# Low-pass block, 16 images: x read a second time in 32-token blocks, its transposes on VectorE, and the next image's first pairs between the H filter chunks

## The reference

```python
xs = jnp.einsum('bhwc,dc->bhwd', x, W1) + b1      # 768 -> 192 channels
xs = jax.nn.gelu(xs, approximate=False)
xs = fft_low(xs)          # |inverse FFT of (FFT * centred low-pass mask)| over H and W
xs = jnp.einsum('bhwd,cd->bhwc', xs, W2) + b2     # 192 -> 768 channels
return x + xs
```

## Time and profile before

| | us |
|---|---|
| median of the runs shown | 2677.9 |
| the runs | 2672.61, 2677.9, 6215.89 |
| profiled execution, from first to last instruction | 2680.7 |
| PE busy in it | 2549.4 (95%) |
| VectorE busy | 1833.9 (68%) |
| ScalarE busy | 1350.4 (50%) |
| GpSimd busy | 397.9 (15%) |
| DMA queue, share of 16 engines' span | 59.8% |

### The profile page before, as it was taken

How to read it: one execution, slowest core, us unless ns; L and a number is a source line. 1 busy time by engine, 2 the same in 40 slices (tenths; PEclk the granted TensorE clock), 3 DMA queues, 4 the chain that set the end, 5 groups by cost and what they waited for, 6 DMA issues and landing times.

```text
span 2680.7 us, 53277 instructions
## 1 busy us (share of the span) xinstructions
PE 2549.4 (95%) x16864; PEld 2485.4 (93%) x16864; DVE 1833.9 (68%) x3980; ACT 1350.4 (50%) x3077; POOL 397.9 (15%) x500
## 2 busy tenths in 40 slices
PE   8899898998999989899998999989999899998999
PEld 7799898998989989899898999989999899998999
DVE  6487575775758757587675766757667576675767
ACT  5355454554545545455454545545455454554544
POOL 1102021020211202112020120201202012020120
PEclk9899999999999999999999999999999999999999
DMA  6474664746647466474665846558455584555845
GB/s 207 106 252 138 201 242 114 264 129 200 240 114 261 131 198 242 114 273 129 204 230 129 282 116 215 208 135 298 103 211 202 140 300 99 207 204 145 299 102 221
DMA packets 342566, 509.48 MB, mean 190 GB/s; under 512 B 78418, under 2 KB 210770, under 8 KB 342228
## 3 DMA queue, kind: packets, MB, share of 16 engines
q1 hardware_dynamic: 342228, 505.31, 59.8%
HBM read 253.60 MB, written 251.66 MB: 188 GB/s over the span
## 4 chain that ended last, share of the span: by engine, by line
PE 83%; DMA 6%; SPq 4%; issue 3%; DVE 2%; ACT 2%; DVEq 0%; ACTq 0%
PE ps L400 22%; PE ps L385 12%; PE ps L401 10%; PE ps L472 6%; PE ps L462 6%; PE ps L463 5%; PE ps L469 5%; PE ps L466 5%; DMA xt_hi<-filtered_rows 4%; PE ps L437 3%; SPq L317 2%; PE ps L411 2%; PE ps L445 2%; DMA filtered_rows<-filt 2%; PE ps L413 2%
## 5 line engine op out<-in xcount | busy, mean ns | idle before, releaser
L400 PE MATMUL ps<-w1s,xt_hi 128*128 128x384 f32 x3072 | 980.2, 374 | 0.0
L521 ACT ACTIVATE xt_hi<-ps 128x512 fp32r<-128x512 f32 x768 | 457.7, 598 | 697.8 <-PE ps L385 674.5
L401 PE MATMUL ps<-w1s,xt_lo 128*128 128x192 f32 x3072 | 772.3, 251 | 0.0
L640 DVE TENSOR_TENSOR xt_lo<-ps,xt_hi 128x512 fp32r<-128x512 f32 x768 | 529.8, 691 | 282.4 <-ACT xt_hi L521 279.6
L702 DVE TENSOR_TENSOR xs<-ps,xs 128x384 f32<-128x384 f32 x1024 | 564.5, 556 | 210.9 <-PE ps L472 159.8
L401 PEld LDWEIGHTS ps<-w1s,xt_lo 128*128 128x128 f32 x3072 | 588.0, 191 | 0.0
L400 PEld LDWEIGHTS ps<-w1s,xt_hi 128*128 128x128 f32 x3072 | 578.8, 188 | 0.0
L472 PE MATMUL ps<-w2b_hi,ob 128*128 128x384 f32 x1024 | 357.0, 349 | 42.7 <-DVE ob L693 42.7
L763 POOL TENSOR_TENSOR diff<-hid 128x192 f32<-128x192 f32 x240 | 232.2, 967 | 1016.8 <-ACT hid L529 1016.8
L462 PE MATMUL ps<-w2a_hi,oa_hi 128*128 128x384 f32 x1024 | 361.3, 353 | 20.8 <-DVE xs L702 19.7
L385 PE MATMUL ps<-ident,xs 128*128 128x128 f32 x2304 | 344.1, 273 | 11.2 <-DMA xs<-x_dram 10.6
(11 more groups left out here) (62 smaller groups left out, 3051.3 us busy)
## 6 DMA issues: line engine op xcount, KB each, us to landing
out_dram<-xs SPq DMA_DIRECT2D x127, 1536.0 KB, 9.3
xs<-x_dram SPq DMA_DIRECT2D x80, 1536.0 KB, 7.2
filtered_rows<-filt SPq DMA_DIRECT2D x256, 192.0 KB, 2.0
x_tail<-x_dram SPq DMA_DIRECT2D x32, 1536.0 KB, 8.5
xs<-x_dram SPq DMA_DIRECT2D x32, 768.0 KB, 6.3
xt_hi<-filtered_rows SPq DMA_DIRECT2D x64, 256.0 KB, 5.1
cols_b<-filtered_rows SPq DMA_DIRECT2D x128, 128.0 KB, 5.4
xt_lo<-filtered_rows SPq DMA_DIRECT2D x64, 256.0 KB, 6.4
```

The costliest lines, as they stand in the source:

```text
L400: nc.tensor.matmul(ps_h[t % 2][:, 0:2 * D], hi, w1s[:, k, :], start=k == 0, stop=False)
L401: ins = nc.tensor.matmul(ps_h[t % 2][:, D:2 * D], lo, w1s[:, k, 0:D], start=False, stop=k == KC - 1)
L521: nc.scalar.activation(xt_hi[:, n % XT_SLOTS, :], ps_xt[n % 2][:], ACT.Copy).then_inc(s_xhi, 1)
L640: nc.vector.tensor_tensor(xt_lo[:, n % XT_SLOTS, :], ps_xt[n % 2][:], xt_hi[:, n % XT_SLOTS, :].bitcast(F32), ALU.subtract).then_inc(s_xlo, 1)
```

## The change

x is read twice. The first reading (`load_xq`) goes into `xq`: for each pair of tiles four DMAs, each into 32 partitions. Partition 32j+t holds token t of each of the pair's eight blocks of 32 tokens, with the 192 channels of quarter j, so pieces of 768 bytes. One VectorE transpose of 128 x 768 per tile then turns every 32 x 32 block and leaves channels on the partitions in `xt`; PE no longer transposes, the identity matrix is gone, and W1 is laid out in the matching order. ACT rounds `xt` into `xt_hi` and DVE subtracts, both from SBUF, a whole tile of 768 elements at a time. The second reading (`load_xr`) brings the same tokens, pair by pair, in an eight-slot ring `xr` in which they are added and stored; the copies of the tail tiles are gone.

`hid_sum` and `hid_pre` work on a pair, `add_half` becomes `add_tile`. `hid_lo` and the low part of the first 128 channels of y (`split_a_lo_pair`) move from VectorE to GpSimd; all twelve stores of y are ScalarE's. The scratch rows get one tensor per image, so that rows of the next image can be written while columns of this one are read. The order becomes: for r in 0 to 15, stage A of pair r+3 of image i with stage C of pair r of image i-1; then the four H chunks of image i, with stage A of pairs 0, 1 and 2 of image i+1 behind the first three of them.

The diff, cut to its core:

```diff
-BLOCKS = 4
-UNITS = TILES * KC // BLOCKS
...
+B = 32
+QUADS = P // B
+CQ = C // QUADS
+
+LEAD = 3
+XQ = 4
+XT = 4
+XR = 8
+X_AHEAD = 5
...
+    x_q = x.rearrange("b h w c -> b (h w) c").rearrange("b (m g t) c -> b m t g c", g=2 * QUADS, t=B)
...
-    rows = nc.dram_tensor("filtered_rows", (H, W, D), F32, kind="Internal").ap()
+    rows = nc.dram_tensor("filtered_rows", (IMAGES, H, W, D), F32, kind="Internal").ap()
...
+            def load_xq(i, p):
+                if p >= XQ or later(i):
+                    sp.wait_ge(s_t, TILES * i + 2 * (p - XQ) + 2)
+                for j in range(QUADS):
+                    sp.dma_start(xq[j * B:(j + 1) * B, p % XQ, :, :].rearrange("p t (g c) -> p (t g) c", c=CQ),
+                                 x_q[i, p, :, :, j * CQ:(j + 1) * CQ]).then_inc(s_xq[p % XQ], 16)
+
+            def load_xr(i, p):
+                if p >= XR or later(i):
+                    sp.wait_ge(s_out[p % XR], 16 * (2 * i + p // XR))
...
+                sp.dma_start(xr[:, p % XR, :, :], x_i[:, 2 * p:2 * p + 2, :]).then_inc(s_xr[p % XR], 16)
...
@@ SyncE @@
+            def turn(i, a, c, n):
+                for r in range(PAIRS):
+                    q = r + LEAD
+                    if a and q < PAIRS:
+                        feed(i, q, n)
+                    if c and 3 <= r < 3 + PAIRS - XR:
+                        load_xr(i - 1, r + X_AHEAD)
+                    if c and r >= 1:
+                        store(i - 1, r - 1)
+                    if a and r >= PAIRS - X_AHEAD:
+                        load_xr(i, r - (PAIRS - X_AHEAD))
+                    if a and q < PAIRS:
+                        write_rows(i, q - 1)
+                    if a and q == PAIRS:
+                        write_rows(i, PAIRS - 1)
+                        read_cols(i)
...
+            def mm1_tile(i, t):
...
+                pe.wait_ge(s_xlo, TILES * i + t + 1)
+                if t % 2 == 0 and (t > 0 or later(i)):
+                    pe.wait_ge(s_pre, PAIRS * i + t // 2)
...
+            def mm1_pair(i, q):
+                for t in range(2):
+                    mm1_tile(i, 2 * q + t)
+                if q >= 1:
+                    filter_w_pair(i, q - 1)
+
@@ TensorE @@
+            def turn(i, a, c, n):
+                for r in range(PAIRS):
+                    q = r + LEAD
+                    if a and q < PAIRS:
+                        mm1_pair(i, q)
+                    if c:
+                        out_tile(i - 1, 2 * r)
+                    if a and q == PAIRS:
+                        filter_w_pair(i, PAIRS - 1)
+                    if c:
+                        out_tile(i - 1, 2 * r + 1)
+                    if a and r == PAIRS - 2:
+                        corner_sums(i)
+                for k in range(CHUNKS):
+                    if a:
+                        for v in range(YBANKS):
+                            filter_h_item(i, k, v)
+                    if n and k < LEAD:
+                        mm1_pair(i + 1, k)
...
+            def transpose_tile(i, t):
+                q = t // 2
+                if t % 2 == 0:
+                    dve.wait_ge(s_xq[q % XQ], 16 * QUADS * (PAIRS // XQ * i + q // XQ + 1))
+                nc.vector.transpose(xt[:, t % XT, :], xq[:, q % XQ, t % 2, :]).then_inc(s_t, 1)
+
+            def xt_lo_tile(i, t):
+                dve.wait_ge(s_xhi, TILES * i + t + 1)
+                nc.vector.tensor_tensor(xt_lo[:, t % XT, :, :].rearrange("p c (g t) -> p c g t", t=B),
+                                        xt[:, t % XT, :].rearrange("p (g c t) -> p c g t", c=KC, t=B),
+                                        xt_hi[:, t % XT, :, :].bitcast(F32).rearrange("p c (g t) -> p c g t", t=B),
+                                        ALU.subtract).then_inc(s_xlo, 1)
...
@@ VectorE @@
+            def turn(i, a, c, n):
...
+                    if c and r > 0:
+                        add_tile(i - 1, 2 * r - 1)
...
+                    if mid:
+                        feed_lo(i, q, n, 0)
+                        feed_transpose(i, q, n, 0)
+                    if c and r + 1 < PAIRS:
+                        split_b_lo_pair(i - 1, r + 1)
+                    if mid:
+                        hid_pair(i, q)
+                        feed_lo(i, q, n, 1)
+                    if c:
+                        add_tile(i - 1, 2 * r)
+                    if mid:
+                        feed_transpose(i, q, n, 1)
...
@@ GpSimd @@
+            def turn(i, a, c, n):
+                if c:
+                    split_a_lo_pair(i - 1, 0)
+                for r in range(PAIRS):
+                    if c and r + 1 < PAIRS:
+                        split_a_lo_pair(i - 1, r + 1)
+                    if a and r + LEAD < PAIRS:
+                        hidden(i, r + LEAD)
```

More of the change, by code:

```diff
@@ L196, in later, with wrap @@
             return not isinstance(i, int) or i > 0
[L198 to L227, removed]
+        def wrap(i, q, n):
+            if q < PAIRS:
+                return i, q
+            return (i + 1, q - PAIRS) if n else None
         def y_slot(c, v):
@@ new lines, in _, with feed @@
+            const(w1f, w1t.rearrange("p (k d) -> p k d", d=D), s_w1)
+            load_xq(0, 0)
+            for t in range(2):
+                const(b1_rows[:, t, :], b1.partition_broadcast(P), s_b1_rows)
+            load_xq(0, 1)
+            load_constants()
+            for p in range(2, XQ):
+                load_xq(0, p)
+            for q in range(LEAD):
+                load_xq(0, q + X_AHEAD - 1)
+                if q >= 1:
+                    write_rows(0, q - 1)
+            def feed(i, q, n):
+                ahead = wrap(i, q + X_AHEAD - 1, n)
+                if ahead is not None:
+                    load_xq(*ahead)
@@ new lines, in feed @@
+            def feed(i, q, n, k):
+                ahead = wrap(i, q + 1, n)
+                if ahead is not None:
+                    xt_hi_tile(ahead[0], 2 * ahead[1] + k)
+            for t in range(2):
+                xt_hi_tile(0, t)
+            for q in range(LEAD):
+                for k in range(2):
+                    feed(0, q, True, k)
+                if q >= 1:
+                    stage_filtered(0, q - 1)
+                gelu_pair(0, q)
+            set_up_at = {0: set_up_w2a_hi, 1: set_up_w2b_hi, 2: set_up_corner}
@@ L587, in turn @@
                 if a:
[L588 to L590 removed]
                     split_hi_pair(i, 0)
[L593 removed]
+            turn(0, True, False, True)
+            with act.Fori(1, IMAGES - 1) as i:
+                turn(i, True, True, True)
+            turn(IMAGES - 1, True, True, False)
+            turn(IMAGES, False, True, False)
         @block.vector
@@ new lines, in feed_transpose @@
+            def feed_transpose(i, q, n, k):
+                ahead = wrap(i, q + 2, n)
+                if ahead is not None:
+                    transpose_tile(ahead[0], 2 * ahead[1] + k)
+            dve.wait_ge(s_w1, 16)
+            link(nc.vector.tensor_copy(w1s[:, :, 0:D], w1f))
+            nc.vector.tensor_tensor(w1s[:, :, D:2 * D], w1f, w1s[:, :, 0:D].bitcast(F32), ALU.subtract).then_inc(s_w1s, 1)
+            for t in range(2):
+                transpose_tile(0, t)
+            for t in range(2):
+                xt_lo_tile(0, t)
+                transpose_tile(0, 2 + t)
```

647 lines of the change are left out of this document (260 added, 387 removed).

## The result

The changed kernel takes 2605.1 us (median of 5 runs, 2602.1 to 2616.2), the kernel before 2677.9. The ratio is 0.974, 95% interval [0.971, 0.977]; it leaves out two disturbed runs of the kernel before (3449 and 6216 us). The direction is right and the time lies in the range of 2250 to 2690, 5 us outside the 2340 to 2600 that the forecast had for itself; the size is a third of the forecast's.

A forecast was written before the change was run, and what follows sets the result against it. PE bound the old kernel; DMA would bind next: 16 x 8.3 + 16.7 = 149.5 us per image, plus 1.5, T = 151. 191.4 + 15 x 151 = 2456, so 2450 us, 8.5% faster; own range 2340 to 2600, overall 2250 to 2690.

The forecast's parts named there:

- hidden-blocks rival: First-reading loads: 768-byte pieces at 325 GB/s, DMA pair 6.9 us, VectorE sets the pace; 2281 us, chance 0.22.
- GpSimd's exclusion: VectorE with two SBUF inputs and GpSimd reading SBUF exclude each other; 0.4 us taken per pair, 0.7 at most.
- the 1.5 us for SP: Added per image because SP empties the DMA queue, waiting for the last rows before it reads columns.
- the sign that was to decide: Pairs with stages A and C: forecast wrong if the DMA share stays under 0.85 there.
- The other sign: Pairs with stages A and C: block loads' time to landing above 10 us would show the forecast.
- two pairs ahead of their transpose: SP's block loads, queued behind `write_rows`: asked for 15 us early, which covers the wait for ScalarE.
- 8.8 us of `out_tile`s: First H chunk: five `out_tile`s on PE cover queue, row write and first columns, 7.0 us before any latency.
- the other 12 us were waits: Period before the change, 166.0 us: PE's work with transposes was 154, the rest waits.
- The moved pairs don't fill the boundary: Image boundary: PE waits for first columns, each period loses some 7 us; T = 158, 2558 us, chance 0.08.
- Slow transposes: VectorE: transposes at 1.90 us each, or GpSimd's exclusion, need 9.7 us per pair; 2649 us, no change, chance 0.12.
- blocks at 100 GB/s: First-reading loads into 32 partitions: rate halves again, a pair's blocks take 7.9 us; 3400 us, slower, chance 0.13.
- the 110.0 that were left alone: Time before the first image's first H filter matmul, 110.0 us, part of the unchanged 191.4, bounds 15 us either way.

The follow-up runs named there:

- all mended: Changed kernel with early blocks, pairs ahead of their H chunks, loop written out and one eighth of the block pieces: 2238.6 us, ratio 0.839.
- experiment 3: Changed kernel with the next image's first three pairs behind all four H chunks on PE and ScalarE: 2591.7 us, ratio 0.971.

## Why the size was wrong

The experiments form a square (ratio to the kernel before):

| | loop and order as changed | early blocks, pairs first, loop written out |
|---|---|---|
| all blocks | 0.974 | 0.901 |
| one eighth of the blocks' bytes | 0.908 | 0.839 |

Rows differ by 6.6 and 6.2 points, columns by 7.3 and 6.9, alike within the intervals of some 0.3 points to either side: two costs that add. In points of 2678 us, traffic is 166 to 177 us and order with loop 184 to 196. With neither, 2239.

- **PE and VectorE: right, slightly too dear.** The hidden-blocks rival gave 2281 with joint pairs at 7.8 us; at the measured 7.5 the same sum gives 191.4 + 15 x (13 x 7.5 + 38) = 2224, measured 2239. The period of that kernel is 135.3 us, the sum's 135.5. The transpose, taken at 0.95 us between 0.51 and 1.90, takes 0.968; `add_tile` 0.942 against 0.95. GpSimd's exclusion shows in `xt_lo`: 0.951 in the median, 1.117 in the mean, 0.33 us for two against the 0.4 taken. Of the 208 that took over 1 us, 204 began while GpSimd's `hid_lo` or `split_a_lo_pair` was running; of the 304 shorter ones none did.
- **The bytes: right.** Taken 205 GB/s, measured 222. The forecast's DMA sum without the 1.5 us for SP is 191.4 + 15 x 149.5 = 2434 us; with order and loop mended the kernel takes 2398 and 2406. The Trainium skill (SBUF — State Buffer, "Door 1: The DMA port swizzle") has 32 or 64 partitions reach half of the ports, up to 218 GB/s. The trace agrees within 2%: 222 against 324 over 128 partitions with the same pieces. Where DMA is paid for was wrong: not in the joint pairs (7.5, not 8.3, at a share of 1.07) but later. Rows land in 7.7 us in the median, before in 2.0, and at the boundary shown in 10.5. So the sign that was to decide, a DMA share under 0.85 in the joint stage, could not tell: the share was as forecast, and the loss lay outside that stage. The other sign, block loads landing in over 10 us there, failed: they landed in 3.6 to 9.
- **The boundary: wrong, and this is the step that failed.** The prediction said that blocks "are asked for two pairs ahead of their transpose, 15 us, which covers it", and for SP's wait "I add 1.5". Two pairs ahead holds inside an image. At the boundary the request stands behind the wait for the rows and sixteen column reads, and the 15 us are gone: blocks asked for at 940.9 were needed near 943 and came at 956.6. Nor was the 1.5 us enough for the queue, whose work was to fill the period: it runs at a share of 0.71 for 11 us, which by the joint pairs' 1.07 loses 11 x (1 - 0.71 / 1.07) = 3.7 us, an estimate, in that window alone. Undoing this alone gave 3.8 points. Nor did 8.8 us of `out_tile`s cover the columns, taken at 7.0: the wait for the rows alone is 10.5. The prediction had the block loads behind `write_rows`, but not behind `read_cols`, which the change puts ahead of those of the next image.
- **The loop's jump: a second failed step, not in the sum at all.** It was in the rows: "issue 3%" of the chain in the earlier trace rows is 80 us, 38 of them at the jumps and 21 in all left with the loop written out, and the prediction read nothing from it. It wrote of the 166.0 us of a period that "the other 12 us were waits" and let them go with the transposes. More than half of them, 6.7 us, were the jump with the slow clock behind it, which the change keeps; in the changed kernel, whose queue is fuller, it is 8.9. Undoing it gave 4.8 points.
- **The clock follows.** The same 13,792 matmuls are busy 2254.6 us in the changed kernel (granted clock 0.929) and 2156.6 with all mended (0.994). So of the 377 us between the two spans 279 are idle time and 98 are matmuls that take longer; windows like that at 956 us, at a clock of 0.50 behind idle time, show where. The sum had no term for it.
- **The rivals.** "The moved pairs don't fill the boundary" (0.08, 2558 us) is what happened, and more: its wait for columns is there, 107.7 / 16 = 6.7 us against "some 7", and experiment 3 shows that the pairs gain nothing there. But its 6.7 us are about a quarter of the 25.3 by which the period, 160.6 us, stands above the 135.3 of the kernel with all edits and an eighth of the block bytes; late blocks, the jump and the clock are the rest. Slow transposes and blocks at 100 GB/s are out. The first image took 11.4 us more than the 110.0 that were left alone, inside the 15 us of its bounds; its cause was not tried.

## What to carry to other kernels

When a change takes the bound engine's work away, list every wait of its period in the trace of before, and say of each whether the change removes it: what isn't on the list stays, and is paid again. On an in-order queue "asked for n steps ahead" has to be checked at the place where the queue waits, not in the steady state; moving the loads of two pairs past one wait was worth more here than the whole change had gained. An "issue" wait in the chain that returns once per iteration can be the loop itself; write the loop out once and measure.

## What the runs showed that was not expected

- Writing out the loop saves 6.7 us per period in the kernel before (DMA share 59.8%) and 8.9 in the changed one (98.2%). With the loop kept and an eighth of the block bytes, ScalarE idles 3.5 us at a jump instead of 8.1.
- DMA work of some 8 us per pair (2.56 MB at the 317 GB/s of the window) doesn't slow pairs of 7.5 us: the queue carries the rest to the next wait for a DMA.
- With 128 partitions, pieces of 768 bytes instead of 3072 cost 0.8% of the time (2479.1 against 2460.4); 32 partitions in four DMAs cost 5% more (2605.1).
